# Attention: both narrow groups of column sums at the seventh beat

## The reference, cut to what matters

```python
def _L1_xattn_ref(q, k, v):
    N_HEAD = 8
    b, d, m = q.shape
    c = v.shape[1]
    h = N_HEAD
    qh = q.reshape(b * h, d // h, m)
    kh = k.reshape(b * h, d // h, -1)
    vh = v.reshape(b * h, c // h, -1)
    scale = 1.0 / jnp.sqrt(jnp.asarray(d // h, dtype=q.dtype))
    qk = jnp.einsum('bdm,bdn->bmn', qh, kh) * scale
    sm = jax.nn.softmax(qk, axis=-1)
    ret = jnp.einsum('bmn,bcn->bcm', sm, vh)
    return ret.reshape(b, c, m)
```

## Time and profile before

| | |
|---|---|
| runs | 1622.52, 1624.83 and 1631.50 us; median 1624.83 us |
| profiled execution, span from first to last instruction | 1622.8 us |
| profiled execution, its own time outside the trace | not listed apart from the runs; the span lies between the lowest run and the median, 2.0 us under the median |
| PE busy over the span | 94% |
| DVE, ACT, POOL busy over the span | 73%, 60%, 64% |
| attention stage, first second of unit 0 to the last sums | about 544 to 1035 us of the span |

### The profile page before, as it was taken

How to read it: one execution, slowest core, us unless ns; L and a number is a source line. 1 busy time by engine, 2 the same in 40 slices (tenths; PEclk the granted TensorE clock), 3 DMA queues, 4 the chain that set the end, 5 groups by cost and what they waited for, 6 DMA issues and landing times.

```text
span 1622.8 us, 28609 instructions
## 1 busy us (share of the span) xinstructions
PE 1524.7 (94%) x8929; PEld 1067.6 (66%) x8929; DVE 1189.2 (73%) x1868; ACT 981.3 (60%) x1529; POOL 1031.2 (64%) x855
## 2 busy tenths in 40 slices
PE   4999999998887999999999999888999999999996
PEld 3677777777554644444444444378999998999985
DVE  7788888888827777777777776275777777777774
ACT  6433333334724478888888877746777766766773
POOL 3788888885307588888888887502555555555553
PEclk8999999999998999999999999999999999999998
DMA  7344444445763967777776872581444444444443
GB/s 256 108 131 134 136 142 142 142 132 131 207 176 110 211 163 188 200 187 187 198 190 185 201 188 68 178 303 29 78 78 78 79 78 79 79 78 73 75 77 52
DMA packets 111131, 224.27 MB, mean 138 GB/s; under 512 B 12992, under 2 KB 12992, under 8 KB 110144
## 3 DMA queue, kind: packets, MB, share of 16 engines
q1 hardware_dynamic: 94560, 185.10, 40.3%
q0 software_dynamic: 15904, 37.23, 13.2%
q10 hardware_dynamic: 576, 0.79, 0.2%
HBM read 146.71 MB, written 75.84 MB: 137 GB/s over the span
## 4 chain that ended last, share of the span: by engine, by line
PE 33%; DMA 24%; issue 4%; DVE 4%; ACT 2%; POOL 1%; SPq 0%; ACTq 0%; POOLq 0%; DVEq 0%
DMA out_rows<-XN,slots 22%; PE pB L1471 10%; PE pO L1481 8%; PE pA L1453 7%; PE pO L1494 4%; PE pO L1645 1%; DMA XN<-normed_rows,slots 1%; PE pA L1633 1%; PE pB L1462 1%; PE pA L1549 1%; POOL out_rows L1435 1%; DVE low L1827 1%; DVE XN L2010 0%; DMA qs<-q_low 0%; DVE XN L1944 0%
## 5 line engine op out<-in xcount | busy, mean ns | idle before, releaser
L1827 DVE TENSOR_REDUCE low<-pA 128x2 f32<-128x1024 f32 x256 | 307.0, 1223 | 109.4 <-PE pA L1453 95.8
L1722 ACT ACTIVATE pt<-pB 128x512 f32<-128x512 f32 x512 | 287.7, 594 | 89.7 <-PE pB L1471 81.1
L1435 POOL DMA_INDIRECT out_rows<-XN,slots x71 | 196.9, 2773 | 217.9 <-DMA out_rows<-XN,slots 170.1
L436 PE MATMUL y<-kv,toep 128*128 128x288 f32 x1280 | 326.0, 411 | 9.0 <-DVEq L63 5.8
L436 PEld LDWEIGHTS y<-kv,toep 128*128 128x128 f32 x1280 | 238.0, 190 | 96.8 <-DVEq L63 34.0
L1633 PEld LDWEIGHTS pA<-XN,fc 128*128 128x128 f32 x2272 | 265.6, 192 | 10.9 <-issue 5.6
L1633 PE MATMUL pA<-XN,fc 128*128 128x128 f32 x2272 | 266.4, 276 | 5.0 <-DVE XN L1990 4.0
L1471 PE MATMUL pB<-qs,ks 98*128 98x512 f32 x512 | 226.9, 446 | 3.3 <-ACT pt L1722 2.4
L1471 PEld LDWEIGHTS pB<-qs,ks 98*128 98x128 f32 x512 | 95.6, 188 | 192.2 <-ACT pt L1722 149.2
L406 ACT ACTIVATE ym<-y 128x384 f32<-128x384 f32 (+1 forms) x128 | 52.6, 411 | 228.9 <-PE y L436 228.9
L1787 ACT ACTIVATE proj_high<-WP 128x2048 fp32r x71 | 135.7, 1912 | 83.6 <-PE pO L1645 83.6
(11 more groups left out here) (294 smaller groups left out, 2448.4 us busy)
## 6 DMA issues: line engine op xcount, KB each, us to landing
ks<-ctx_high SPq DMA_DIRECT2D x62, 256.0 KB, 4.6
qs<-q_high SPq DMA_DIRECT2D x62, 256.0 KB, 6.1
kc<-in_ctx_conv SPq DMA_DIRECT2D x32, 384.0 KB, 5.5
XN<-in_x SPq DMA_DIRECT2D x16, 512.0 KB, 9.8
toep<-kernel_and_skip SPq DMA_DIRECT2D x32, 256.0 KB, 3.5
ct<-in_ctx SPq DMA_DIRECT2D x16, 512.0 KB, 6.6
ctx_high<-kh SPq DMA_DIRECT2D x16, 512.0 KB, 4.5
ctx_low<-kl SPq DMA_DIRECT2D x16, 512.0 KB, 5.2
```

The lines of the kernel that those rows point to most:

```text
L436: m = pe.matmul(y[half].rearrange("p (l n) c -> p l n c", l=CB)[:, l, :, 0:PAIRS], toep[u][:, (l - s) * P:(l - s + 1) * P], kv[u][:, half, ...
L1435: pool.indirect_dma_start(out=out["out"], out_offset=bass.IndirectOffsetOnAxis(ap=slots[:, j:j + 1], axis=0), in_=ys[j % 2], in_offset=Non ...
L1722: act.activation(pt[s][:, h, :], bank(u, n), ACT.Exp, scale=SCALE1).then_inc(s_exp, 1)
L1827: dve.tensor_reduce(ap(low[u % 2], t % CB * NH + t // CB, [[NH, 2], [1, 1]]), pA[n % 2], op=ALU.max, axis=AX.X, negate=True).then_inc(s_re ...
```

## The change

The two calls of `sums` become one, at the seventh beat: first the three waits, then the four heads with `part_sum`, then the four with `pt[3]`. Each group still counts up `s_sum` when it is done. Behind the last unit both groups stood together already; there the three waits move ahead of both.

```diff
-            def sums(j, u, last):
-
-                if last:
-                    pe.wait_ge(s_exp, made(j, place(j, CB - 1, NH - 1)))
-                else:
-                    pe.wait_ge(s_add, 4 * j + 4)
-                    wait(pe, s_att, j)
-                rows = pt[CB - 1] if last else part_sum
-                for h in range(NH):
-                    m = pe.matmul(pO[(u + 1) % 2][h * HD1:(h + 1) * HD1, :], ones, rows[:, h, :], start=not last, stop=last)
-                m.then_inc(s_sum, 1)
+            def sums(j, u):
+
+                pe.wait_ge(s_add, 4 * j + 4)
+                wait(pe, s_att, j)
+                pe.wait_ge(s_exp, made(j, place(j, CB - 1, NH - 1)))
+                for rows, last in ((part_sum, False), (pt[CB - 1], True)):
+                    for h in range(NH):
+                        m = pe.matmul(pO[(u + 1) % 2][h * HD1:(h + 1) * HD1, :], ones, rows[:, h, :], start=not last, stop=last)
+                    m.then_inc(s_sum, 1)
 
             def finish(j, i, u, beat):
 
                 if beat == 2:
                     values(j, i, u, 2)
-                if beat == 5:
-                    sums(j, u, False)
                 if beat == 7:
-                    sums(j, u, True)
+                    sums(j, u)
                 if beat == 10:
                     values(j, i, u, 3)
...
-            sums(UNITS - 1, TRIP - 1, False)
-            sums(UNITS - 1, TRIP - 1, True)
+            sums(UNITS - 1, TRIP - 1)
```

## The result

| | before | after |
|---|---|---|
| median of 16 runs each | 1626.02 us (1621.56 to 1631.50) | 1632.89 us (1626.67 to 1637.22) |
| ratio of the runs, 95% interval | | 1.0043 (1.0029 to 1.0056) |
| span of the profiled execution | 1622.8 us | 1630.1 us |
| a unit in the loop, mean of the 24 units 4 to 27 | 364.52 / 24 = 15.189 us | 368.25 / 24 = 15.344 us |
| start of unit 1 to start of unit 31 | 455.61 us | 460.56 us |

The kernel became slower by 0.43%, which is 4.7 to 9.1 us; the forecast was 5.1 us and 0.3%. The change lies within the 0.5% that the prediction called "no change", but 16 runs on each side are enough to tell it from 1. The argument can be read again in one unit of the changed kernel.

The account below looks back on a forecast made before the run. The prediction took PE's order of work in the attention as the bound. 29 units at +0.15 us and two at +0.38 us sum to +5.1 us, giving 1629.9 us on the median; range 1618 to 1636 us.

Parts of the forecast that it names:

- Step (1): PE at beat 7: a group directly behind another costs 0.85 us, against 1.20 alone; -0.34 us a unit.
- Step (2): Beats 3 to 7, no narrow group: seconds 6 and 7 wait for exponentials 4 and 5, losing 0.25 and 0.23 us.
- Step (3): Score 6 also waits for a DVE reduction; costs nothing, since second 7's own bound is 0.10 us later.
- Step (4): POOL's part sums, `norm` and the logarithm around the later first sums: no cost; POOL gets 0.15 us more room.
- Step (5): Three waits in PE's queue before one pair instead of two groups: nothing, at the most 0.35 us.
- Step (6): Units 30 and 31, where no scores fill the wait: +0.38 us in each.
- The rival in which the saving stays whole: In the loop, ACT keeps up or seconds 6 and 7 needn't wait: 10.5 us less, 1614.3 us; chance 0.10.
- The rival of half a stall: Each wait in a unit costs only half: -0.10 us a unit, 3 us less, 1621.7 us; chance 0.14.
- The dear pair: In the loop the pair's second group costs 1.20 us like the first: +15.2 us, 1640.0 us; chance 0.12.

Follow-up runs that it names:

- the other pair pulled apart: Kernel before, score order and `measure` changed, values of slice 2 at beat 2, part sums at beat 3 (adjoining at beat 3: 14.907 us): 15.215 us a unit, 1.0018.
- the run with both short: Changed kernel with exponentials 4 and 5 and DVE's reduction of the pair 2 and 3 cut to 64 of 512 columns: 14.966 us a unit, ratio 0.9965.
- The repeat: The changed kernel measured again, unaltered, against the kernel before: 15.349 us a unit, attention +5.08 us, ratio 1.0060 (1.0039 to 1.0080).

## Why the prediction was right, and where it was short

**The forecast** was 1629.9 us and +5.1; measured are 1632.89 us and a ratio worth 7.0 us (4.7 to 9.1). Of the 3.0 us between 1629.9 and 1632.89, 1.2 are the median before, which is 1626.02 over 16 runs where the three known ones had 1624.83; the rest, 1.8, is what stays open below. The sign and the mechanism were right, and so was the size of what the prediction described: 4.95 us in the attention and 0.38 in unit 31.

- Step (1), the group behind a group for 0.85 in place of 1.20: measured 1.86 us for the pair, 0.851 us a unit with a third group, 0.31 with the other pair pulled apart. Right.
- Step (2), the waits of seconds 6 and 7: the loads start 0.05 us after the ends of exponentials 4 and 5; second 3 to second 8 takes 4.89 us, as written beforehand; the unit 15.344 for 15.34. Together they are worth 0.48 us by the run with one group and the late `measure`. Right.
- Step (3), score 6 behind DVE with 0.10 us of cover: its load starts at 812.18 - 810.13 = 2.05 us after second 3, as worked out (808.08 - 806.03), and the cover is 0.09 us a unit by the run with short exponentials. Right, and it mattered more than the step said: it is the second lock on the same saving.
- Step (4): POOL's adds start 0.19 us earlier against second 3, forecast were 0.15; they wait for the first sums, as foreseen. `norm` is done at 814.33, more than a microsecond before the next exponential.
- Step (5), nothing for the three waits: the run with a third group has them too and pays 0.851. Right.
- Step (6), +0.38 us each in units 30 and 31: unit 31 takes 3.46 us from second 5 to second 8 (1026.01 to 1029.47), the figure that the step comes to (1022.77 - 1019.31); unit 30 is 14.82 us for 14.42.

**The rival in which the saving stays whole** was given 0.10 and its price was 31 x 0.34 us. The runs show that it was further off than the prediction said: it needed not only a quicker ACT but also DVE out of the way (15.258 with short exponentials, 14.966 with both). The view that would have said so stood in the trace of before, in the reduction that score 6 needs; the prediction used it as a cover and did not ask what it would do to the rival. Nor did it see DVE's `measure`, which holds the unit at 15.135 us when PE has a whole group less. In the run with both short the reduction ahead of `measure` is shorter as well, and the unit goes below that. **The rival of half a stall** is out: each load came where the prices put it. **The dear pair** is out by the third group.

**What stays open** is about 2 us. From the start of unit 1 to that of unit 31 the change costs 5.0 us, and unit 31 adds 0.4; 16 runs say 4.7 to 9.1 in all, which holds that sum. The repeat says 6.3 to 13, and the version with beat 7 reordered 3.7 to 10.2 where the attention has 2.5; these two don't. The profiles can't place the rest. Outside the attention they differ from one another by more than 2 us, in both directions: unit 1 starts at 559.8 us in the profile of before and between 560.8 and 566.4 in all the others, and from the start of unit 31 to the end it is 602 to 609 us. In unit 0 of before the load of a score waits 1.77 us for a transfer. The runs' granted clock says a little more. Over the 35 runs of before beside the repeat, the time falls by about 0.9 us for each 0.001 of mean granted clock (an estimate, a line through these runs). Their mean clock is 0.981, that of the repeat and of the reordered version 0.979. By that line it makes some 1.9 of the 9.4 us between the means of the repeat and of before, and 1.7 of the 6.3 of the reordered version: about half of what the attention leaves over. In the loop the granted clock is 1.00, so this part lies outside it. Why the clock was lower, and whether the rest is chance or comes from the altered program, is not shown; neither is part of the forecast's mechanism.

## What to carry to other kernels

A saved switch in an engine's stream is worth what the next bound leaves of it: before joining two pieces of work, count the row of short pieces that forms where one was taken out, and hold it against the slowest consumer of its double buffer, and against the second slowest too. In a hand-written order the expensive piece may be the pause that a neighbour needs, and two groups side by side cost 0.8 us a unit at one beat (the sums at beat 6) and save 0.3 at another (values and part sums at beat 3). Prices of a wait read from one row each (release to load, load to end) were enough here to give the length of a unit to within 0.01 us in all but two of the runs (0.055 and 0.07 off), which an average of busy time could not.

## What the runs showed that was not expected

- A group of eight narrow matmuls, 1.20 us of PE's stream, could be removed for a gain of 0.05 us a unit, because DVE's two short instructions of `measure` (0.68 and 0.18 us, but 1.36 us from the start of the first to the next reduction) hold the reduction behind them.
- Putting the score ahead of the second in one beat took 0.095 us a unit (15.344 to 15.249) with the same instructions: what fills a wait need not follow it.
- The page's busy share of PE was 94% before and after, and 100% in the loop in both, through a change of 1% in the unit. Idle stretches of 0.2 to 0.3 us in the weight loads (811.80 and 812.18 in the changed kernel) don't appear as idle time of PE.
